# Four layers on one core: bias rows as products of a row of ones, banks read in place, values copied by ScalarE

## What is computed

```python
# layer 0: attention with 16 heads of 64, then a feed-forward
x = x + g_msa * (attention(...) @ W_out + b_out)
# layer 1: 16 heads of 8, rotary positions
q = (nx @ wq + bq).reshape(b, s, 16, 8)          # k with bk, v with bv likewise
q = q * c + _rotate_half(q) * si                 # k likewise, v not
attn = softmax(q k^T / sqrt(8)) @ v
x = x + attn @ wo + bo
nx = _ada_rmsnorm(x, ...)                        # then a gated feed-forward
# layer 2: a quantised recurrent layer and its feed-forward
# layer 3: linear attention, 16 heads of 8
q = softmax(xn @ Wq + bq, axis=-1)               # over the 8 features of a head
k = softmax(xn @ Wk + bk, axis=1)                # over the tokens
ctx = einsum('bnhd,bnhl->bhdl', k, xn @ Wv + bv)
y = einsum('bnhd,bhdl->bnhl', q, ctx)
h = layer_norm(y, sn_g, sn_b) * (1.0 + scale) + shift
return x + cond * (silu(h) @ out_W + out_b)
```

## Time and profile before

| | |
|---|---|
| time, median of 3 runs | 510.35 us (509.69 to 513.29) |
| time of the profiled execution | 511.04 us |
| its span | 509.2 us |
| mean granted TensorE clock | 0.848 of full |
| PE busy | 388.8 us (76%), 2489 instructions |
| DVE busy | 324.6 us (64%), 797 instructions |
| ACT busy | 271.6 us (53%), 748 instructions |
| POOL busy | 135.8 us (27%), 162 instructions |

### The profile page before, as it was taken

The page is one execution under the profiler, slowest core; times in us unless marked ns, Lnnn a source line. Parts: engine busy times, 40 slices in busy tenths (PEclk is TensorE's granted clock), DMA queues, the critical chain, the costliest instruction groups (busy, mean ns, idle before and its releaser), DMA issues.

```text
span 509.2 us, 7326 instructions
## 1 busy us (share of the span) xinstructions
PE 388.8 (76%) x2489; PEld 251.9 (49%) x2489; DVE 324.6 (64%) x797; ACT 271.6 (53%) x748; POOL 135.8 (27%) x162
## 2 busy tenths in 40 slices
PE   4989999989999979778898798789991531155564
PEld 4656567567567666445455454445461421004343
DVE  4447888655777833795956647422269259878884
ACT  1475564699697625357364443465421861286342
POOL 1043343343354712100507300001003013371101
PEclk9999999999999997978888957997897555555796
DMA  8950000000000000000000000000000000000001
GB/s 313 448 205 1 1 0 3 1 2 2 0 2 1 1 2 1 0 0 2 0 1 1 1 1 2 1 1 1 1 0 0 1 1 0 1 0 1 1 0 41
DMA packets 3835, 13.25 MB, mean 26 GB/s; under 512 B 372, under 2 KB 2420, under 8 KB 3284
## 3 DMA queue, kind: packets, MB, share of 16 engines
q1 hardware_dynamic: 3800, 12.80, 6.3%
HBM read 12.28 MB, written 0.52 MB: 25 GB/s over the span
## 4 chain that ended last, share of the span: by engine, by line
PE 60%; DVE 21%; ACT 8%; issue 6%; POOL 2%; DMA 1%; POOLq 0%; SPq 0%; ACTq 0%; DVEq 0%
PE bank L955 7%; PE bank L935 6%; PE bank L982 6%; PE bank L969 6%; PE bank L1106 4%; PE bank L940 3%; DVE tab_ L1428 3%; PE bank L1053 3%; PE bank L1001 3%; DVE area L1428 3%; PE bank L1187 2%; PE bank L1208 2%; PE bank L1282 2%; ACT area L532 2%; ACT big L532 2%
## 5 line engine op out<-in xcount | busy, mean ns | idle before, releaser
L532 ACT ACTIVATE big<-bank 128x512 f32<-128x512 f32 (+1 forms) x104 | 53.0, 530 | 64.2 <-PE bank L1192 43.7
L532 ACT ACTIVATE area<-bank 128x512 f32<-128x512 f32 (+3 forms) x68 | 37.0, 551 | 48.9 <-PE bank L940 16.4
L456 POOL TENSOR_TENSOR big<-big,rrec 128x512 f32<-128x512 f32 x44 | 44.8, 1040 | 67.3 <-DVE rrec L1629 67.3
L1613 DVE TENSOR_REDUCE nmax<-bank 128x2 f32<-128x512 f32 x64 | 43.4, 679 | 29.4 <-PE bank L955 29.2
L1574 DVE TENSOR_REDUCE nmax<-bank 128x2 f32<-128x512 f32 x64 | 42.4, 681 | 30.7 <-PE bank L1165 30.6
L1621 DVE COPY area<-bank 128x512 f32<-128x512 f32 x64 | 42.5, 683 | 9.4 <-PE bank L969 8.6
L532 ACT ACTIVATE big<-bank,nmax 128x256 f32<-128x256 f32 x88 | 41.0, 478 | 12.1 <-PE bank L935 8.1
L935 PE MATMUL bank<-xT,w0s 128*128 128x256 f32 x128 | 33.9, 396 | 5.8 <-issue 5.8
L955 PE MATMUL bank<-area 64*128 64x256 f32 x256 | 36.3, 402 | 0.0
L982 PE MATMUL bank<-area 128*64 128x256 f32 x256 | 34.7, 391 | 0.6 <-ACT big L532 0.6
L1297 PE MATMUL bank<-identb,area 128*128 128x128 bf16 x40 | 5.9, 309 | 34.5 <-DVE area L1431 34.5
(11 more groups left out here) (237 smaller groups left out, 869.9 us busy)
## 6 DMA issues: line engine op xcount, KB each, us to landing
w2s<-w SPq DMA_DIRECT2D x1, 4352.0 KB, 26.8
rows<-row SPq DMA_DIRECT2D x1, 1600.0 KB, 10.9
w0s<-w SPq DMA_DIRECT2D x3, 512.0 KB, 6.8
w1s<-w SPq DMA_DIRECT2D x1, 1408.0 KB, 15.8
w0s<-w SPq DMA_DIRECT2D x1, 1024.0 KB, 12.9
xs<-x SPq DMA_DIRECT2D x1, 512.0 KB, 4.2
out<-tab_ SPq DMA_DIRECT2D x2, 256.0 KB, 2.3
tabs<-tab SPq DMA_DIRECT2D x1, 423.5 KB, 5.2
```

What stands on the lines that cost most here:

```text
L456: pool.tensor_tensor(prob[n % SLOTS], prob[n % SLOTS], rrec0[:, n % 4, :].unsqueeze(2).to_broadcast([P, QT, SEQ]), ALU.mult).then_inc(S("a ...
L532: return nc.scalar.activation(o, i, f, **kw)
L1613: V.tensor_reduce(nmax0[:, n % 4, :], bank[n % 4][:, :].rearrange("p (q k) -> p q k", q=QT), AX, ALU.max, negate=True).then_inc(S("a0_max" ...
```

## The change

Bias rows become products. `row_first` writes the bias into a bank by a product of one row of ones with the bias row, and the real product adds to it. This is done for `b_out` in layer 0's last batch, for q, k and v in the rotary stage and for `bo` in half 1 of layer 1's output. DVE then reads the bank in place. In the rotary stage q and k go by one product of 256 columns per tile (`turning`), into banks 2 to 5; the values of a half go into one bank (`values_in`), and ACT copies them (`values_out`). Of the sixteen copies of the parts DVE takes the two numbered 13 and 15 (`KEPT`). In layer 3 the queries and values of half 0 are made ahead of the keys, those of half 1 behind; the bias of q is one DVE addition per half, the bias of v comes in by a second set of products in `contexts` (keys times bias row, all 128 rows), ACT copies the values, and its table of exponentials is loaded ahead of the layer. Statistics and layer norm of `y` read the banks. `out_W` times the condition is made early by POOL (`w3c`), so that the last product needs only the addition of `xs`, and the additions of condition and `out_b` to `xs` come behind the norm `n3y`.

```diff
+        KEPT = (4 * NB - 3, 4 * NB - 1)
+        def part_taken(n):
+            if n in KEPT:
+                return S("a1_kept"), KEPT.index(n) + 1
+            return S("a1_taken"), n + 1 - sum(k < n for k in KEPT)
...
+            for b in range(NB):
+                m = pool.tensor_tensor(w3c[:, b, :], part(w3s, W3, "out"), part(rows, ROW, "cond", b * P, (b + 1) * P),
+                                       ALU.mult)
+            m.then_inc(S("w3_cond"), 1)
...
+            def values_out(half):
+                act.wait_ge(S("a1_vmm"), half + 1)
+                acti(vtm[:, 4 * half:4 * half + 4, :, 0:DH1], two(half).rearrange("p t (h d) -> p t h d", d=DH1), ACT.Copy
+                     ).then_inc(S("a1_v"), 1)
             act.wait_ge(S("x_ready"), 2)
             squares("n1a", 1, lambda t: xs[:, t, :], junk1)
+            act.wait_ge(S("v_zero"), 2)
+            values_out(0)
             modulated("n1a", 1, lambda b: ada1[:, 0, b:b + 1], lambda b: ada1[:, 1, b:b + 1])
...
+                if b == 2:
+                    values_out(1)
...
+                        if n in KEPT:
+                            continue
...
+            acti(ks[:, 0:1], magic[:, 0:1], ACT.Exp, scale=0.0)
...
+            values3(0)
+            keys3(0)
+            keys3(1)
+            exp_queries(0)
+            exp_keys(0)
+            exp_keys(1)
+            keys_turned(0)
             exp_queries(1)
+            values3(1)
+            keys_turned(1)
...
-                act.wait_ge(S("l3_y"), half + 1)
-                acti(ta[:, 4 * half:4 * half + 4, :], two(half), ACT.Copy).then_inc(S("l3_ys"), 1)
...
+            def row_first(o, name, a=0, b=None):
+                mm(o, ones[0:1, :], part(rows, ROW, name, a, b)[0:1, :], start=True, stop=False)
...
+                last = b == NB - 1
...
+                if last:
+                    row_first(bank[7][:, 0:P], "b_out")
+                pe.wait_ge(S("w0_in"), 16)
+                pe.wait_ge(S("a0_aT"), 8 * b + 8)
                 for q in range(QT):
+                    if last and q:
+                        row_first(bank[7][:, q * P:(q + 1) * P], "b_out")
                     for c in range(8):
                         m = mm(bank[7][:, q * P:(q + 1) * P], aT[:, c, q * P:(q + 1) * P],
-                               part(w0s, W0, "out", c * P, (c + 1) * P), start=(c == 0), stop=(c == 7))
+                               part(w0s, W0, "out", c * P, (c + 1) * P), start=(c == 0 and not last), stop=(c == 7))
...
-            for t in range(TT_):
+            def turning(t):
+                if t >= 4:
+                    pe.wait_ge(S("a1_qk"), t - 3)
+                row_first(bank[2 + t % 4][:, 0:2 * P], "bqkv1", 0, 2 * P)
                 if t % QT == 0:
                     pe.wait_ge(S("xT"), 2 * NB + t // QT + 1)
-                if t == 4:
-                    pe.wait_ge(S("x_ready"), 2)
-                if t >= 6:
-                    pe.wait_ge(S("a1_qkv"), t - 5)
-                mm(bank[(t + 2) % 6][:, 0:3 * P], xT[:, t * P:(t + 1) * P], part(w1s, W1, "qkv"), start=True,
-                   stop=True).then_inc(S("a1_qkvmm"), 1)
-                if t == 3:
-                    normed_T("n1a", 1)
+                mm(bank[2 + t % 4][:, 0:2 * P], xT[:, t * P:(t + 1) * P], part(w1s, W1, "qkv", 0, 2 * P), start=False,
+                   stop=True).then_inc(S("a1_qkmm"), 1)
+            def values_in(half):
+                pe.wait_ge(S("xT"), 2 * NB + 2 * half + 2)
+                pe.wait_ge(S("x_ready"), half + 1)
+                for t in half_of(half):
+                    row_first(two(half)[:, t % 4, :], "bqkv1", 2 * P, 3 * P)
+                    m = mm(two(half)[:, t % 4, :], xT[:, t * P:(t + 1) * P], part(w1s, W1, "qkv", 2 * P, 3 * P),
+                           start=False, stop=True)
+                m.then_inc(S("a1_vmm"), 1)
+            for t in range(4):
+                turning(t)
+            values_in(0)
+            normed_T("n1a", 1)
+            for t in range(4, TT_):
+                turning(t)
+            values_in(1)
...
+                    if half:
+                        row_first(to[:, (t % 4) * P:(t % 4 + 1) * P], "bo1")
                     m = mm(to[:, (t % 4) * P:(t % 4 + 1) * P], aT1[half][:, (t % 4) * P:(t % 4 + 1) * P],
-                           part(w1s, W1, "wo"), start=True, stop=True)
+                           part(w1s, W1, "wo"), start=not half, stop=True)
...
+            def queries_values(half):
+                pe.wait_ge(S("xT"), 4 * NB + 2 * half + 2)
+                for i, tag in ((0, "l3_qmm"), (1, "l3_vmm")):
+                    for t in half_of(half):
+                        m = mm(two(2 + 2 * i + half)[:, t % 4, :], xT[:, t * P:(t + 1) * P],
+                               part(w3s, W3, "qkv", i * P, (i + 1) * P), start=True, stop=True)
+                    m.then_inc(S(tag), 1)
+            queries_values(0)
             for half in range(2):
                 pe.wait_ge(S("xT"), 4 * NB + 2 * half + 2)
                 mm(bank[half][:, :], part(w3s, W3, "qkv", 2 * P, 3 * P), xT[:, half * 512:half * 512 + 512],
                    start=True, stop=True).then_inc(S("l3_kmm"), 1)
-            for t in range(TT_):
-                mm(bank[2 + t // 2][:, (t % 2) * 2 * P:(t % 2 + 1) * 2 * P], xT[:, t * P:(t + 1) * P],
-                   part(w3s, W3, "qkv", 0, 2 * P), start=True, stop=True).then_inc(S("l3_qv"), 1)
+            queries_values(1)
...
-                               start=(k == 0), stop=(k == QT - 1))
+                               start=(k == 0), stop=False)
+                    for k in range(QT):
+                        m = mm(two(2 + 3 * half)[:, b, :], tb[:, b * QT + k, :], part(rows, ROW, "bqv3", P, 2 * P),
+                               start=False, stop=(k == QT - 1))
...
-                m = mm(two(t // 4)[:, t % 4, :], xT[:, t * P:(t + 1) * P], part(w3s, W3, "out"),
+                m = mm(two(t // 4)[:, t % 4, :], xT[:, t * P:(t + 1) * P], w3c[:, t // QT, :],
...
+                if b < NB - 1:
+                    tt(yb[:, :, :], src, row_bc(part(rows, ROW, "b_out"), QT), ALU.add).then_inc(S("a0_y"), 1)
+                    dve.wait_ge(S("a0_y"), b + 1)
+                    src = yb[:, :, :]
+                link(tt(yb[:, :, :], src, row_bc(gates[:, b, 0, :], QT)))
+                if b == NB - 1:
+                    dve.sem_inc(S("a0_y"), 1)
...
-                dve.wait_ge(S("a1_qkvmm"), t + 1)
-                tt(vtm[:, t, :, 0:DH1], bank[(t + 2) % 6][:, 2 * P:3 * P].rearrange("p (h d) -> p h d", d=DH1),
-                   part(rows, ROW, "bqkv1", 2 * P, 3 * P).rearrange("p (h d) -> p h d", d=DH1), ALU.add)
-                tt(qk[:, t % 2, :], bank[(t + 2) % 6][:, 0:2 * P], part(rows, ROW, "bqkv1", 0, 2 * P),
-                   ALU.add).then_inc(S("a1_qkv"), 1)
-                dve.wait_ge(S("a1_qkv"), t + 1)
-                tt(roped(t), heads(qk[:, t % 2, :], 0, 8), table(t, "cos", 0, 8))
+                dve.wait_ge(S("a1_qkmm"), t + 1)
+                qk = bank[2 + t % 4][:, 0:2 * P]
+                tt(roped(t), heads(qk, 0, 8), table(t, "cos", 0, 8))
                 if t >= 1:
                     dve.wait_ge(S("a1_rope"), t)
-                tt(heads(turned, 0, 4), heads(qk[:, t % 2, :], 4, 8), table(t, "sin", 0, 4))
-                link(tt(heads(turned, 4, 8), heads(qk[:, t % 2, :], 0, 4), table(t, "sin", 4, 8)))
+                tt(heads(turned, 0, 4), heads(qk, 4, 8), table(t, "sin", 0, 4))
+                tt(heads(turned, 4, 8), heads(qk, 0, 4), table(t, "sin", 4, 8)).then_inc(S("a1_qk"), 1)
+                dve.wait_ge(S("a1_qk"), t + 1)
                 tt(roped(t), roped(t), heads(turned, 0, 8), ALU.add).then_inc(S("a1_rope"), 1)
...
+            for n in KEPT:
+                dve.wait_ge(S("a1_part"), n + 1)
+                V.tensor_copy(part_place(n), bank[6 + n % 2][:, :].rearrange("p (g t) -> p g t", g=2)
+                              ).then_inc(S("a1_kept"), 1)
...
-                link(tt(xn[:, h4, :], src, row_bc(part(rows, ROW, "bo1"), 4), ALU.add))
-                tt(xs[:, h4, :], xs[:, h4, :], xn[:, h4, :], ALU.add).then_inc(S("x_ready"), 1)
+                if half == 0:
+                    link(tt(xn[:, h4, :], src, row_bc(part(rows, ROW, "bo1"), 4), ALU.add))
+                    src = xn[:, h4, :]
+                tt(xs[:, h4, :], xs[:, h4, :], src, ALU.add).then_inc(S("x_ready"), 1)
...
+            def queries_top(half):
                 hs = heads_of(half)
-                for t in half_of(half):
-                    dve.wait_ge(S("l3_qv"), t // 2 * 2 + 2)
-                    src = bank[2 + t // 2][:, (t % 2) * 2 * P:(t % 2 + 1) * 2 * P]
-                    tt(big[:, t * P:(t + 1) * P], src[:, P:2 * P], part(rows, ROW, "bqv3", P, 2 * P), ALU.add)
-                    m = tt(ta[:, t, :], src[:, 0:P], part(rows, ROW, "bqv3", 0, P), ALU.add)
-                m.then_inc(S("l3_v"), 1)
-                dve.wait_ge(S("l3_v"), half + 1)
```

(27 more changed lines are left out.)

66 lines of the change are left out of this document (28 added, 38 removed).

## The result

The changed kernel takes 530.0 us (median of 4 runs), the kernel before 510.57 (median of 4 runs beside them). The ratio is 1.0425, 95% interval 1.0382 to 1.0468; the two medians alone give 1.038. It is slower by some 19 us by the medians, where 508.3 had been forecast. The profiled execution of the changed kernel is 529.54, its span 527.7 (before 509.2), so 18.5 longer.

A forecast was written before the change was run, and what follows sets the result against it. Mostly TensorE (PE 60%, DVE 21%, ACT 8%), but DVE without a gap in the rotary stage. Terms −0.2 − 2.0 + 1.6 − 1.4 = −2.0, off the median 510.35: 508.3 us; eight in ten runs from 503 to 513.5.

The forecast's parts named there:

- Layer 0's last batch: Output product: DVE's bias add goes, two one-row products come in, one hidden, one costing 0.24; net −0.2 us.
- POOL's products: Four `w3c` products ahead of the deviation of `n1a`, under 4.2 us, hidden in POOL's idle 12.95; cost zero.
- The rotary stage: DVE gives back 4.5 us, added work on PE and ACT eats 2.5; scores begin at 236.5, not 238.52: −2.0.
- the walk through the rest: Rotary stage's second half: first part in its bank at 223.1, then ACT's copies and the takes, scores at 236.5.
- Rival A: One-row products let the clock fall in the rotary stage: +4 us there, 514.4 in all; chance 0.17.
- The output half: Layer 1, half 1: PE is the chain, DVE's saved add buys nothing, four row products cost +1.6 us.
- Layer 3: ACT's copy of `y` goes (−0.65), fewer DVE operations at the end (−0.7), the middle gains nothing: −1.4 us.
- the 4.1 assumed: Layer 3's `contexts`: twice the products, 32 passes in 4.1 us where 16 took 2.05.
- B: Every saving of DVE arrives and PE's and ACT's added work hides: −7.5, so 502.9 us; chance 0.18.
- C: Some bank reads are dearer, some 65 of 412 ns, in rotary stage and layer 3: +0.1, 510.5 us; chance 0.15.
- DVE's 4.5: Rotary stage: 0.56 us less DVE work on each of eight tiles, 4.5, the bound on the good side.

The follow-up runs named there:

- e11: Changed kernel with bias products of 64 rows in place of one, so those biases count 64 times: 519.97 us, ratio 1.0172 to the kernel before.
- e1: Changed kernel with bias products of 128 rows (identity times bias rows) in place of one row: 509.5 us, ratio 0.9973 to the kernel before.
- e10: Kernel before with the rotary stage alone changed, its bias products of 128 rows: 508.54 us, ratio 0.9936.
- e4: Changed kernel with rotary stage and layer 1's output half as before; layers 0 and 3 and POOL's products changed: 510.96 us, ratio 0.9991.
- e5: Kernel without the computation, only stretches of PE products of various row counts: 0.22 us each at 128 rows, 0.42 by turns with fewer, at full clock.
- e6: e1 with layer 1's output half and layer 0's last batch as before: 507.05 us, ratio 0.9940 to the kernel before.
- e2: Changed kernel without bias products in the rotary stage and for `bo`, so biases are missing: 506.5 us, ratio 0.9944 to the kernel before.
- e3: Changed kernel with one-row products grouped: four ahead of four products, one of 512 columns for values and `bo`: 515.78 us, ratio 1.0127 to the kernel before.
- e12: e6 with DVE copying the second half's values, their products moved behind the first four transposed parts: 504.46 us, ratio 0.9892 to the kernel before.

## Why the prediction was wrong, step by step

**Layer 0's last batch:** −0.2 forecast, +0.3 measured. One row product among full ones was put at 0.24 and cost 0.41, the two halves around it took 4.02 in place of 3.82, and DVE waited 0.1 more behind them.

**POOL's products:** nothing, as forecast; no chain has them.

**The rotary stage:** −2.0 forecast, +15.1 measured. This is the step that failed, and it did at the line "By the 0.24 above, 256 columns are some 0.45 and a half is 4 × 0.9 + 4 × 0.48 = 5.5". The 0.24 is from a row in which products of one shape follow each other; nothing in it shows a change of shape. By turns with one row a half costs 8.3 even at the full clock (four pairs of 0.63 and four of 0.41), as e11 shows, and with the clock at 0.50 it took 15.0 (223.79 to 238.78). By e11 and e1 the +15.1 is 5.5 to 6.0 for the turns and 11.6 to 12.1 for the clock, less the 2.5 that e1's stage is under the one of before. The loss came in both halves: the transposes of `n1a` 1 were 5.6 later in the stage, and from them to the first part it took 9.0 more. With the 5.5 assumed, the walk through the rest held: in e1 and e10, whose products cost 0.43 and 0.22, the stage is 2.5 shorter than before, where 2.0 was forecast, and ACT's copies and the transposes set its end. A part of that is luck: the same code as before took 27.49 in e4, against which it is 1.4, and the clock, at 0.50 for some of the stage before, stayed at 1.00 in e1. That DVE's reading of a bank costs nothing was right here: `area<-bank,tabs` 128x128 took 279 ns, from SBUF 284.

**Rival A** named the cause that decided, from the rows with 4 rows at 0.50, and gave it 0.17 and +4. It deserved more, though the trace of before couldn't settle it: in 354:355 PE was busy 1.00 with 4 rows and the clock at 0.50, but in 361:362 it was busy 1.00 with 4 rows again and the clock at 1.00, and in 358:359 busy 1.00 with 128 rows at 0.50. A run like e5 would have. Its price was too small by the other fault, since at half speed it took 0.90 and 0.48 for a product where 1.15 and 0.72 were measured, and it slowed the second half of the stage alone. The rule of the Trainium skill that the gate follows how busy PE is (TensorE: Matmul & The Clock Gate, Part 1) would have excluded it; e5 shows PE busy 4.00 of 4.00 us with one row and the clock at 0.50, so the measurement decides against it.

**The output half:** +1.6 forecast, +3.5 measured; the mechanism (PE is the chain, DVE's saved add buys nothing) was right, the size is off by the turns again: eight products in 5.26, at 0.72 each but the first two, in place of 1.69 + 1.6. With 128 rows and the clock at 0.50 too they took 3.55 (e1), so 1.7 of the 3.6 is the turns.

**Layer 3:** −1.4 forecast, −1.55 by the trace (32.28 to 30.73). Its products have 128 rows on both sides. `contexts` took 3.7 in place of the 4.1 assumed. One item was dearer: the layer norm that reads a bank, 1.38 for the last four in place of 1.13. The runs don't confirm the gain: e4's ratio can't be told from 1, and e6 and e10 differ by it and not in their ratios.

**Rivals B and C.** B didn't come: e2, which has no bias products in this stage, has a stage of 26.08, so 2.4 of DVE's 4.5 arrived, and 3.1 if the clock had not cost it its lead over e1. C didn't come for the rotary stage's products and for the statistics, but it did for the eight operations of the layer norm, 62 ns each, 0.5 in all; it is hidden in layer 3's total.

**Still open** is the attention's +1.7. Its instructions are the same; in the changed kernel the clock was low in other stretches of it, and over all profiled executions its length lay between 107.2 and 110.8 whatever the change. I take it for the clock's phase, which no run isolates.

## What to carry to other kernels

A product with a short contraction isn't cheap on PE because it is small. By turns with full ones it and each of its neighbours cost 0.42 in place of 0.22, and in number such products went with the clock at 0.50, under which everything beside them is slow too. Where a bias is to be added by a product, use all rows (identity times the copied bias rows); put together, the short ones cost less, but e3 was still 1.3% slower than the kernel before. Even with all rows the change is worth little as it stands (e1, 0.3%); e12 gets its 1.1% with the output half and layer 0 left as before and the values' products moved off the way of the first transposes. Cost an added instruction from a row in which its neighbours are those it will have, or measure it alone first.

## What the runs showed of the hardware that I had not expected

- A change of the number of rows from product to product costs 0.2 for each at the full clock (e5: 0.42 in place of 0.22, 128 columns, f32), the same for 1, 32 and 64 rows against 128. With 128 rows throughout it is 0.22 although the stationary (the operand that is loaded as weights) changes each time; no run keeps it fixed.
- With PE busy 4.00 of 4.00 us the clock was at 0.50 for products of one row and for 1 and 32 rows by turns with 128, and at 1.00 for 64 rows, for 64 by turns with 128 and for 128 (e5).
- The layer norm's `xn<-bank,mv,area` 128x128 took 400 ns, where `xn<-tab_,mv,area` took 338; two-operand products and statistics showed no such difference (279 and 284; 284 and 280). By the table of the Trainium skill, VectorE: DVE Perf Modes, section on the TRN2 errata, a bank as source costs 62 cycles of 0.96 GHz more, by estimate 65 ns. The one form agrees with it (62 ns), the others don't.
- Bias products of 128 rows, 16 pairs in the rotary stage, cost that stage little, but not nothing: about 0.7 by the traces of e1 and e2 up to the point where e2's clock fell.
